# Two residual layers with picked weights: rows transposed by VectorE squares and SBUF transfers, `up` in plain float32, the root by a GpSimd power, `out` nine tiles behind `down`

## The reference

```python
h = relu(x @ W1[id0] + b1[id0])                 # 512 -> 128
a = x + h @ W2[id0] + b2[id0]                   # 128 -> 512
n = (a - mean(a)) * rsqrt(var(a) + 1e-5)        # over the 512 columns
x1 = x + n * gamma[id0] + beta[id0]
out = x1 + x1 @ W[id1] + b[id1]                 # 512 -> 512
```

## Time and profile before

| | |
|---|---|
| time, median of 3 runs | 313.99 us (313.78 to 314.19) |
| span of the profiled execution | 312.3 us |
| its own time | not given apart; 313.99 us less the span leaves 1.7 us around it |
| TensorE busy | 303.9 us, 97% of the span |
| VectorE, ScalarE, GpSimd busy | 225.6, 211.1, 225.8 us |
| granted TensorE clock | 1.00 in every slice (2.4 GHz) |
| bytes moved | 65.39 MB, mean 209 GB/s |

### The profile page before, as it was taken

How to read it: one execution, slowest core, us unless ns; L and a number is a source line. 1 busy time by engine, 2 the same in 40 slices (tenths; PEclk the granted TensorE clock), 3 DMA queues, 4 the chain that set the end, 5 groups by cost and what they waited for, 6 DMA issues and landing times.

```text
span 312.3 us, 4810 instructions
## 1 busy us (share of the span) xinstructions
PE 303.9 (97%) x1424; PEld 244.4 (78%) x1424; DVE 225.6 (72%) x641; ACT 211.1 (68%) x381; POOL 225.8 (72%) x185
## 2 busy tenths in 40 slices
PE   8988999999999999999999999999999999999995
PEld 8424678888888888888888888888888888888884
DVE  0185989696986869598686969778695977889610
ACT  1045667886696958778596857958686874857431
POOL 0649685999779995999959996899959995541000
PEclk9999999999999999999999999999999999999999
DMA  6999795778766798768867888677867381111122
GB/s 199 338 364 370 237 338 176 218 233 284 216 172 212 207 297 250 182 185 258 275 192 197 232 256 247 154 215 246 303 202 198 111 300 37 67 67 71 67 101 101
DMA packets 40943, 65.39 MB, mean 209 GB/s; under 512 B 6100, under 2 KB 10196, under 8 KB 40916
## 3 DMA queue, kind: packets, MB, share of 16 engines
q1 hardware_dynamic: 40336, 64.03, 66.2%
q10 hardware_dynamic: 580, 1.05, 1.1%
HBM read 48.29 MB, written 16.78 MB: 208 GB/s over the span
## 4 chain that ended last, share of the span: by engine, by line
PE 92%; DVE 4%; ACT 2%; issue 1%; POOL 0%; POOLq 0%
PE out_ps L778 54%; PE down_ps L778 14%; PE h_ps L778 13%; PE turn_ps L833 9%; PE turn_ps L904 2%; DVE y L488 1%; ACT y L376 1%; DVE stats L493 1%; DVE turn_ps L532 0%; DVE x1T_lo L539 0%; ACT w_hi L347 0%; ACT hT L358 0%; ACT out_sb L394 0%; DVE mean_var L497 0%; ACT w_hi L341 0%
## 5 line engine op out<-in xcount | busy, mean ns | idle before, releaser
L778 PE MATMUL out_ps<-x1T_hi,w_hi 128*128 128x512 f32 x256 | 100.4, 392 | 0.0
L778 PE MATMUL out_ps<-x1T_lo,w_hi 128*128 128x512 f32 x256 | 99.8, 390 | 0.0
L778 PE MATMUL out_ps<-x1T_hi,w_lo 128*128 128x512 f32 x256 | 99.7, 389 | 0.0
L687 POOL TENSOR_TENSOR xrow<-xrow,b_rows 128x512 f32<-128x512 f32 x64 | 82.6, 1294 | 9.3 <-DMA xrow<-x_rows 9.3
L385 ACT ACTIVATE x1T_hi<-turn_ps,gamma_beta 128x512 fp32r<-128x512 f32 x64 | 43.2, 689 | 43.7 <-DVE turn_ps L532 43.7
L532 DVE SCALAR_TENSOR_TENSOR turn_ps<-turn_ps,gamma_beta,xT 128x512 f32<-128x512 f32 x64 | 45.4, 754 | 34.4 <-PE turn_ps L833 33.5
L376 ACT ACTIVATE y<-y,shift,rstd 128x512 f32<-128x512 f32 x64 | 52.2, 818 | 20.4 <-DVE shift L523 20.0
L692 POOL TENSOR_TENSOR xT_lo<-xT,xT_hi 128x512 fp32r<-128x512 f32 x48 | 62.4, 1300 | 4.7 <-ACT xT_hi L328 4.7
L488 DVE TENSOR_TENSOR y<-down_ps,xrow 128x512 f32<-128x512 f32 x64 | 43.7, 683 | 19.6 <-PE down_ps L778 19.5
L778 PEld LDWEIGHTS out_ps<-x1T_hi,w_hi 128*128 128x128 f32 x256 | 48.1, 188 | 10.9 <-issue 0.8
L778 PEld LDWEIGHTS out_ps<-x1T_hi,w_lo 128*128 128x128 f32 x256 | 48.1, 188 | 10.1 <-issue 0.2
(11 more groups left out here) (40 smaller groups left out, 356.8 us busy)
## 6 DMA issues: line engine op xcount, KB each, us to landing
xrow<-x_rows SPq DMA_DIRECT2D x32, 512.0 KB, 6.7
out_cols<-out_sb SPq DMA_DIRECT2D x64, 256.0 KB, 2.6
xT<-x_cols SPq DMA_DIRECT2D x30, 512.0 KB, 6.2
w<-w_all SPq DMA_DIRECT2D x8, 1024.0 KB, 7.2
w<-w_all SPq DMA_DIRECT2D x15, 256.0 KB, 5.2
b_rows<-b_all SPq DMA_DIRECT2D x8, 256.0 KB, 8.1
xT<-x_cols ACTq DMA_DIRECT2D x4, 256.0 KB, 4.6
w<-w_all SPq DMA_DIRECT2D x4, 64.0 KB, 3.7
```

The source lines that it names most:

```text
L687: nc.gpsimd.tensor_tensor(xrow[:, i % XR, :], xrow[:, i % XR, :], b2_rows[:, m % 2, :], ALU.add).then_inc(rowbias_done, 1)
L778: mm = nc.tensor.matmul(out, lhsT, rhs, start=first and n == 0, stop=last and n == len(terms) - 1)
```

## The change

The first two blocks (tiles 0 to 7, `SQUARED`) keep their TensorE transposes. From the third on `square(i)` transposes each 32x32 square of a normalised tile on VectorE into `squares`, with the columns of the four tiles of a block interleaved; sixteen SBUF to SBUF transfers a block (`move`, on the SP queue, 64 KB each in pieces of 512 bytes) bring the squares to their partitions in `normT`. For the interleave a tile takes every fourth row of its block: the rows are loaded so, and `relu` writes the hidden values so. `merge` reads `normT` in place of `turn_ps`, and its first of a block waits for all sixteen transfers. `merge` and `x1_low` lie in the steps with s % 4 of 3 and 0, `move` in those with 1. `up` is one plain float32 product everywhere, and the splits of x and W1 are gone. From tile 11 on `add_eps` on VectorE and `inverse_root` on GpSimd take the place of `standard` and the reciprocal with its Newton step. `out` lies nine tiles behind `down`, with no `out` in steps 13 and 15. The columns are loaded 8 tiles ahead, not 10.

```diff
+    LOAD_COLS, LOAD_ROWS = 8, 6
+    UP = 5
     BIAS_ROWS = 3
     DOWN = 0
     NORM = -1
-    OUT = -7
-    FINISH = -8
-    LAST = TILES - 1 - FINISH
-    PLAIN_UP, PLAIN_DOWN = 2 * PER, PER
-    OPEN = 11
+    OUT = -9
+    LAST = TILES - OUT
+    PLAIN_DOWN = PER
+    SQUARED = 2 * BLOCK
+    POWER = OPEN = 11
+    Q = 32
...
+        first = {3: s - 7, 0: s - 6}.get(s % BLOCK, -1)
+        return (first, first + 1) if first >= SQUARED and there(first) else ()
+    def out_of(s):
+        i = {7: 0, 8: 1, 9: 2, 10: 3, 11: 4, 12: 5, 13: -1, 14: 6, 15: -1, 16: 7}.get(s, s + OUT)
+        return i if there(i) else None
+    def moved(s):
+        blk = (s - 5) // BLOCK
+        return blk if s % BLOCK == 1 and SQUARED <= blk * BLOCK < TILES else None
     with ExitStack() as ctx:
...
+                if i < SQUARED:
...
+                    rows = x_rows[first * P:first * P + NB, :].rearrange("(p t) d -> p t d", t=BLOCK)[:, t:t + 2, :]
+                sp.dma_start(xrow[:, i % XR:i % XR + 2, :], rows).then_inc(rows_in[i // 2 % (XR // 2)], 16)
...
+            def move(blk):
+                sp.wait_ge(square_done, BLOCK * (blk + 1) - SQUARED)
+                sp.wait_ge(merge_done, BLOCK * blk)
+                for q in range(KC):
+                    for j in range(KC):
+                        source = squares[Q * q:Q * (q + 1), blk % 2].rearrange("a (k j) r -> a k j r", j=KC)[:, :, j, :]
+                        sp.dma_start(normT[Q * j:Q * (j + 1), :, q * P:(q + 1) * P], source).then_inc(moved_in[q], 16)
...
             def step(s):
+                if moved(s) is not None:
+                    move(moved(s))
...
+                by_tile, by_column = hT[:, blk % 2, :], h_ps[blk % 2][:]
+                if blk * BLOCK >= SQUARED:
+                    by_tile = by_tile.rearrange("a (t q) -> a t q", t=BLOCK)
+                    by_column = by_column.rearrange("a (q t) -> a t q", t=BLOCK)
+                nc.scalar.activation(by_tile, by_column, ACT.Relu, bias=b1[:, m:m + 1]).then_inc(relu_done, 1)
...
             def step(s):
-                for i in turned(s):
-                    x1_high(i)
-                if there(s + FINISH):
-                    finish(s + FINISH)
+                if out_of(s - 1) is not None:
+                    finish(out_of(s - 1))
+                if there(s + NORM):
+                    normalise(s + NORM)
                 if (s + UP) % BLOCK == BLOCK - 1 and there(s + UP):
                     relu((s + UP) // BLOCK)
-                if there(s + XHI):
-                    x_hi(s + XHI)
+                for i in merged(s):
+                    x1_high(i)
                 if (s + UP) % BLOCK == BLOCK - 1 and there(s + UP):
                     h_high((s + UP) // BLOCK)
-                if there(s + NORM):
-                    normalise(s + NORM)
...
+            def add_eps(i):
+                r = slice(i % WR, i % WR + 1)
+                dve.wait_ge(mean_var_done, i + 1)
+                nc.vector.tensor_scalar(var_eps[:, r], mean_var[:, i % WR, 1:2], EPS, None, ALU.add
+                                        ).then_inc(vareps_done, 1)
...
+            def square(i):
+                blk, t = i // BLOCK, i % BLOCK
+                dve.wait_ge(norm_done, i + 1)
+                nc.vector.transpose(squares[:, blk % 2, :, t::BLOCK], y[:, i % WR, :]).then_inc(square_done, 1)
...
-                dve.wait_ge(turn_done, i + 1)
+                gamma, blk = i % KC, i // BLOCK
+                if i < SQUARED:
+                    dve.wait_ge(turn_done, i + 1)
+                else:
+                    dve.wait_ge(x1lo_done, i - 1)
+                    if i % BLOCK == 0:
+                        for q in range(KC):
+                            dve.wait_ge(moved_in[q], 16 * KC * (blk + 1 - SQUARED // BLOCK))
                 if i % PER == 0:
                     dve.wait_ge(gamma_beta_in[i // PER], 16)
-                nc.vector.scalar_tensor_tensor(turn_ps[i % 2][:], turn_ps[i % 2][:],
+                normed = turn_ps[i % 2][:] if i < SQUARED else normT[:, i % KC, :]
+                nc.vector.scalar_tensor_tensor(turn_ps[i % 2][:], normed,
                                                gamma_beta[:, i // PER, gamma:gamma + 1],
                                                xT[:, i % XC, :], ALU.mult, ALU.add).then_inc(merge_done, 1)
...
+                normed, new, first, second = s + NORM, s + DOWN, *(merged(s) or (None, None))
+                if there(normed) and normed < POWER:
+                    rstd_start(normed)
+                    rstd_newton(normed)
+                    rstd_end(normed)
+                if there(normed):
+                    mean_shift(normed)
+                if there(new):
+                    add_rows(new)
+                if first is not None:
+                    merge(first)
+                if there(new):
+                    statistics(new)
+                if second is not None:
+                    merge(second)
+                if there(new):
+                    mean_variance(new)
+                if first is not None:
+                    x1_low(first)
+                if there(new):
+                    add_eps(new)
+                if second is not None:
+                    x1_low(second)
+                if there(normed):
+                    square(normed)
...
+            def inverse_root(i):
+                r = slice(i % WR, i % WR + 1)
+                pool.wait_ge(vareps_done, i - POWER + 1)
+                nc.gpsimd.tensor_tensor(rstd[:, r], var_eps[:, r], neg_half[:], ALU.pow).then_inc(rstd_done, 1)
...
+                if there(s):
+                    inverse_root(s)
...
+                wait_cols(pe, i)
+                if i < KC:
+                    pe.wait_ge(w1_first_in[k], 16)
+                if i % PER == 0 and m >= 1:
+                    pe.wait_ge(w1_in[m % 2], 16 * ((m + 1) // 2))
...
+                product(h_ps[blk % 2][:], [(w1[:, m % 2, k], xT[:, i % XC, :])], first=k == 0, last=k == KC - 1
+                        ).then_inc(up_done, 1)
...
             def step(s):
-                for i in turned(s):
-                    turn(i)
                 if there(s + DOWN):
                     down(s + DOWN)
                 if there(s + UP):
                     up(s + UP)
-                if there(s + OUT):
-                    out(s + OUT)
+                if out_of(s) is not None:
+                    out(out_of(s))
```

More of the change, by code:

```diff
@@ L59, in w_part, with merged @@
         return m, part if 0 <= m < SAMPLES and -1 <= part < KC else None
-    def turned(s):
-        first = {1: s - 5, 2: s - 4}.get(s % BLOCK, -1)
-        return (first, first + 1) if there(first) else ()
+    def merged(s):
+        first = {3: s - 7, 0: s - 6}.get(s % BLOCK, -1)
[6 more added lines that the diff above has]
+        return blk if s % BLOCK == 1 and SQUARED <= blk * BLOCK < TILES else None
     with ExitStack() as ctx:
@@ L84, in cond_resid_kernel @@
         y = sb("y", [P, WR, D])
+        squares = sb("squares", [P, 2, D // Q, P])
+        normT = sb("normT", [P, KC, NB])
         x1T_hi = sb("x1T_hi", [P, WR, NB], f32r)
@@ L110, in cond_resid_kernel @@
         rstd0 = sb("rstd0", [P, WR])
+        var_eps = sb("var_eps", [P, WR])
+        neg_half = sb("neg_half", [P, 1])
         newton = sb("newton", [P, WR])
@@ L136, in cond_resid_kernel @@
         up_done, down_done, turn_done, out_done = (sem(n) for n in ("up_done", "down_done", "turn_done", "out_done"))
-        xhi_done, xlo_done = sem("xhi_done"), sem("xlo_done")
+        square_done = sem("square_done")
+        moved_in = [sem(f"moved_in{q}") for q in range(KC)]
         relu_done, hhi_done, hlo_done = sem("relu_done"), sem("hhi_done"), sem("hlo_done")
@@ L241, in load_rows @@
                     sp.wait_ge(y_done, i + 2 - XR)
-                sp.dma_start(xrow[:, i % XR:i % XR + 2, :],
-                             x_rows[i * P:(i + 2) * P, :].rearrange("(t p) d -> p t d", p=P)
-                             ).then_inc(rows_in[i // 2 % (XR // 2)], 16)
+                if i < SQUARED:
+                    rows = x_rows[i * P:(i + 2) * P, :].rearrange("(t p) d -> p t d", p=P)
+                else:
+                    first, t = i - i % BLOCK, i % BLOCK
+                    rows = x_rows[first * P:first * P + NB, :].rearrange("(p t) d -> p t d", t=BLOCK)[:, t:t + 2, :]
+                sp.dma_start(xrow[:, i % XR:i % XR + 2, :], rows).then_inc(rows_in[i // 2 % (XR // 2)], 16)
             def store(i):
@@ L300, in step @@
                     load_b(s // PER)
-                if there(s + FINISH):
-                    store(s + FINISH)
+                if s >= 8 and out_of(s - 1) is not None:
+                    store(out_of(s - 1))
             opening()
@@ L357, in relu @@
                     act.wait_ge(hlo_done, blk - 3)
-                nc.scalar.activation(hT[:, blk % 2, :], h_ps[blk % 2][:], ACT.Relu, bias=b1[:, m:m + 1]
```

(43 more changed lines are left out.)

71 lines of the change are left out of this document (12 added, 59 removed).

## The result

| | before | changed |
|---|---|---|
| median of the runs | 313.88 us (313.39 to 314.19, 4 runs) | 388.0 us (387.26 to 388.95, 4 runs) |
| ratio, 95% interval | | 1.237 (1.2335 to 1.2401) |
| span of the profiled execution | 312.3 us | 385.5 us |
| mean granted clock of TensorE | 1.0 | 0.916 |

The kernel became 24% slower. The direction was forecast and the size was not: 322.6 us had been predicted and 334 was the upper end of the range, so 388.0 lies 54 us outside it.

A forecast was written before the change was run, and what follows sets the result against it. TensorE was taken to bound the kernel before, the loop through the move the changed one. T = 88.8 + 2L + 12(M + L) gave 320.9 us of span, 322.6 us with 1.7 around it; range 306 to 334, the forecast's own 316 to 328.

The forecast's parts named there:

- L: Time from a block's last square through semaphore, issues and landing to the next first merge: 8.9 us, between 7.4 and 9.9.
- M: VectorE's time from the first merge of a block to the end of its last square: 9.1 us.
- The loop: First merge, squares, sixteen transfers, next first merge: period M + L of 18.0 us, expected to set the end.
- What bounds it and what TensorE gains: TensorE bounds the kernel before; its block falls from 18.11 to 17.1 us, with plain `up` at 0.87 us.
- The landing: Last transfer of a move, from issue to landing: 2.2 us, bounds 1.6 and 2.6.
- The issue: Price of each transfer issued in a row on SP's queue: 0.44 us, bounds 0.38 and 0.48.
- The square: VectorE's 32x32 transpose of a normalised tile: 0.66 us, other bound 1.3 us for its strided writes.
- rival 3: The square on VectorE costs twice, 1.3 us for 0.66: 338 us in all; chance 0.07.
- The root: GpSimd's power for the reciprocal root: 0.3 us, hidden, costing nothing up to 1 us.
- Rival 2: Merges reading two SBUF operands wait for GpSimd: 0.8 us a period, 332 us in all; chance 0.17.
- Rival 1: The move is short enough, L of 7.7 us, so the kernel gets faster: about 307 us; chance 0.30.
- The late column load: Column loads issued behind the move land after two steps, so TensorE waits at `up`; would make all forecasts wrong.

The follow-up runs named there:

- e3: The changed kernel with each of the sixteen transfers moving one run of 2 KB per partition in place of four pieces of 512 bytes; 382.8 us.
- e4: The changed kernel with `square` issued ahead of the second merge in VectorE's step; 381.7 us.
- e6: The changed kernel with four of a block's sixteen transfers issued and twelve left out; 349.4 us.
- e11: The changed kernel with the root first in GpSimd's step and the transfers split, ten by SP and six by ScalarE; 344.2 us.
- e9: The changed kernel with the reciprocal root issued first in GpSimd's step; 385.4 us.
- e10: The changed kernel with four of a block's sixteen transfers and the root issued first in GpSimd's step; 327.8 us.

## Why the prediction was wrong in size

The failed step is the price of an issue: "I take 0.44, nearest to those in a row; bounds 0.38 ... and 0.48". It measured 0.645 in an undisturbed move and 0.67 in the mean of all. The sum of the forecast was T = 88.8 + 2L + 12(M + L), so L counts 14 times. Its 320.9 us of span against 385.5 leave 64.6 us:

| term | forecast | measured | times | us |
|---|---|---|---|---|
| fifteen issues | 6.6 | 10.0 | 14 | 48 |
| rest of L (semaphore, landing and the wait for it) | 2.3 | 2.2 | 14 | -1 |
| two squares in M | 1.32 | 1.9 | 12 | 7 |
| rest of M | 7.8 | 7.7 | 12 | -1 |
| root late and merge slow, every second block | 0 | 1.15 | 6 | 7 |
| start: square(11) later | 58.8 | 61.15 | 1 | 2 |
| last M, and the last `out`s at half clock | 8.0 + 20.3 | 8.4 + 22.6 | 1 | 3 |

The sum is 65. Each line is the difference of the two columns times the count, from unrounded times.

- *The loop*: right. The first merge of a block sets the pace, released by the transfers of `normT`, and e3, e4, e6 and e11 move the time as M + L says, as long as no second loop takes over.
- *What bounds it and what TensorE gains*: 0.87 us for a plain `up` was right (0.86), and 0.04 us more went between it and the end of its `out`. The gain on TensorE never appeared: a block is 5.3 us longer than its 17.1 us of work, in pauses and half clock, and not one.
- *The landing*: 2.2 us was right (2.0).
- *The issue*: wrong. The bounds came from transfers that all had HBM on one side; they were bounds of another kind of operation. The trace of before has no SBUF to SBUF transfer, so the upper bound had nothing to stand on, and this should have widened the range. The range was narrower even than these bounds: L = 9.9 gives 198 + 14 x 9.9 = 336.6 us, and it ended at 334.
- *The square*: 0.66 was wrong, 0.93 measured; the bound of 1.3 held, and rival 3 (1.3) had the cause, the stride, right with half its size.
- *The root*: "hidden" was wrong. Its own 0.55 us would have fitted into the 1 us that I had for it; I looked at its duration and not at what is ahead of it in GpSimd's queue. In the changed kernel this costs some 3 us (e9), with the moves out of the way 21.6 (e10).
- *Rival 2*: its mechanism exists (e9), at 0.3 us in every second block of the changed kernel and not 0.8 in each period, since the late root kept the two operations mostly apart. Where the root is early and the moves are short (e10), four merges lose 1.0 us a period, about what the rival said.
- *Rival 1*: fell; it needed L below 8.3 and L is 12.2.
- *The late column load*: there (13.1 us of TensorE's weight loads waiting for `xT` in all), but the chain that ended last names no such wait.

The edits in a ladder, each against its own kernel before: plain `up` +10.6 us; with the power +10.3; with squares, new order and four transfers, root first, +14.2; with all sixteen +71.7; root last, as in the change, +74.1. The twelve other transfers are 57.5 us of it.

Open: why an issue costs more where both sides are of one kind, what holds up single issues of a move for 0.8 to 1.8 us, and whether the slow merges are all of the 0.9 us between e10's period and the 17.5 to 17.8 that was expected.

## What to carry to other kernels

Where an edit brings in a transfer between two memories that the trace doesn't have, the row of a transfer between two others bounds nothing above; count the issues on a loop, because each one's error comes back with the number of transfers times the number of rounds (here 15 x 14). Find the loop (last producer, issue, landing, first consumer, back) before you credit a saving on the busiest engine. And of a small operation given to another engine ask what stands ahead of it in that engine's order, since an in-order queue gives it their delays, be it a root on GpSimd or a transfer on ScalarE.

## What the hardware showed unexpectedly

- An issue on a queue, 64 KB, in a row: 0.64 us SBUF to SBUF (equal for 128 partitions x 512 B and 32 x 2 KB), 0.67 HBM to HBM, 0.47 with HBM on one side. Alone: 0.486 us SBUF to SBUF, 0.332 for a store. Stores of 256 KB in a row: 0.43 at first, 0.69 from the seventh on.
- VectorE's 32x32 transpose of 128x512 float32: a slot of 0.60 us dense, 0.91 with results 16 bytes apart.
- After TensorE's pause of 2 us its granted clock averaged 0.63 and then 0.80 over the next 6 us, and one `out` took 4.41 us for 2.72. In the middle of the kernel this lay beside the move; at the end, behind a pause of 6.35 us, the last part of the kernel took 2.3 us longer than forecast.
- A merge with two SBUF operands took 1.43 us beside a GpSimd subtraction, 0.74 without.
